# Attention scores in groups of four heads: fp32 row groups in place of restacked three-part rows

## The chip, the cores and the metric

The kernel runs on one core of one Trainium2 chip. The metric is the device time of one execution in microseconds (us), less is better. A median over runs is given where several were timed. Engines: TensorE (PE; its weight loads are PEld), VectorE (DVE), ScalarE (ACT), GpSimd (POOL), and the DMA queue that SyncE (SP) issues.

## The reference

A batch of 16 sequences of 512 tokens, width 512, goes through one conditioned transformer layer and a rotation, all in fp32:

```
x = LN(src) * (1 + scale_b) + shift_b            # scale, shift from a time step
q, k, v = x Wq + bq, x Wk + bk, x Wv + bv        # 16 heads of 32
s = q k^T / sqrt(32) + bias[b, h]                # bias: 16 x 16 x 512 x 512, 268 MB
s[mask] = -inf;  p = softmax(s)
x = x + (p v) Wo + bo
h = LN(x) * g2 + beta2
out = rotate(x + gelu2(h W1 + b1) W2 + b2)       # F = 2048; pairs turned by theta, phi
```

## The kernel before

Three stages follow each other: a setup block (weights split into a high and a low part, `WH` and `WL`, and the modulation), `attention_stage`, and `ffn_stage`. The last two run over the 16 batches; attention writes its context and the modulated x to DRAM (`ctx_dram`, `xmod_dram`), and the FFN stage reads them.

Every engine has its own program with its instructions in an order written out by hand. In `attention_stage` the function `body(mode, b)` is emitted for START, FIRST, MIDDLE (a loop), LAST and END, and walks over 64 slots, one per head j and query tile i of 128 queries (`TL` = 64). Counters on semaphores (`Tally`) say which event of which batch an instruction waits for. Scores run `LEAD` = 6 slots ahead of the transposes.

- Precision: x, the weights, q and k are each split into a high and a low part of reduced fp32 (fp32r). A projection of 128 rows is 12 matmuls of 512 columns (`fill`, L654). For the scores, q and k of each head are restacked: `stacked` holds (hi, hi, lo) of q and (hi, lo, hi) of k under each other, 96 rows, so that one fp32r matmul (L699) gives hi.hi + hi.lo + lo.hi. The restacking is done by DMAs: 12 for q of each group of four heads, two stores and three loads through `k_dram` for k (`stack_rows`).
- Per slot: one score matmul into one of two banks; on VectorE the sum with bias, its row minimum (the negated maximum) and the write to a prob buffer in one instruction (L855, called the max below); exp with its row sum on ScalarE (L749); four transposes (L717) of the probabilities of one head and one key tile, across all four query tiles; a copy of the result to `probT` on ScalarE (even i, L744) or VectorE (odd i, L455).
- After each group of four heads: probs.V in four steps of four heads (L681), fp32, each head in its own 32 columns of the array; the row sums are inverted, widened (L889), transposed and multiplied into the context (L895).
- GpSimd adds the mask to the bias (L609), two tiles at a time, in four half buffers that SP refills; it also makes `maskb` once per batch (L598).
- For the next batch: layer norm statistics and the normalization on VectorE (L801, L813), x transposed, then evicted twice by ScalarE as `XH` and `xf` (L774), and the low part `XL` on VectorE (L866). q and k are evicted as hi on ScalarE (L783) and lo on VectorE (L876), V with its bias on VectorE (L871).
- The FFN stage projects the context with Wo (L1181, plain fp32), adds x and bo, and runs the two FFN products as three-part fp32r matmuls (L1172, L1210).

## Time and profile before

| | |
|---|---|
| median of 3 runs | 3711.62 us (3698.89 to 3714.21) |
| span of the profiled execution, the only time given for it | 3722.1 us |
| TensorE, VectorE, ScalarE, GpSimd busy | 93%, 59%, 44%, 46% |
| mean granted TensorE clock | 0.974 of 2.4 GHz |
| DMA | 525 MB, mean 141 GB/s; 240 to 257 GB/s in the attention stage |
| attention stage, FFN stage | about 1945 us, about 1775 us |

Busy shares count the time in which an instruction of the engine is under way. A matmul's record includes its way through the array, and records overlap; the rate of TensorE is read from the distance of starts. Instructions of one engine run in order.

### The profile page before, as it was taken

Reading aid. Unit: us, or ns where it says so; the run is one execution under the profiler, and the core shown is the slowest. Engines: PE = TensorE matmul, PEld = TensorE weight load, DVE = VectorE, ACT = ScalarE, POOL = GpSimd, SP = SyncE. Lnnn points to the kernel's source line nnn. Section 1 sums busy time; section 2 is a strip of 40 time slices with the busy share of each in tenths; the row PEclk is TensorE's granted clock in tenths of the full one; section 3 lists DMA queues with packets and bytes.
Section 4 is the critical chain, followed back from the end, with each engine's and each line's share of the span. In section 5 each row is a group of like instructions: output and inputs, shape, how many; then the busy total and the mean of one; then the engine's idle time right before and its main releaser. Section 6 shows DMA issues by size and latency. Waiting matters only on the chain. (4 is left out here: it accounts for less than half of the span.)

```text
span 3722.1 us, 58023 instructions
## 1 busy us (share of the span) xinstructions
PE 3463.4 (93%) x17344; PEld 2516.1 (68%) x17344; DVE 2202.4 (59%) x4462; ACT 1635.4 (44%) x3493; POOL 1713.3 (46%) x1131
## 2 busy tenths in 40 slices
PE   4998989899899898999978999999999999999998
PEld 3666656666566666666656777777777777777776
DVE  4887778777887777877754443443444344344443
ACT  3666666666776666666652222222222222222221
POOL 1656566566665656656641322333333233333333
PEclk9999999999999999999987999999999999999999
DMA  5888788888888888878762000100000000000100
GB/s 160 257 248 241 239 245 249 240 247 249 254 256 246 242 247 247 246 233 247 237 212 90 35 26 9 35 34 35 34 35 32 26 12 35 35 35 35 35 6 18
DMA packets 296179, 525.06 MB, mean 141 GB/s; under 512 B 36672, under 2 KB 44864, under 8 KB 295488
## 3 DMA queue, kind: packets, MB, share of 16 engines
q1 hardware_dynamic: 296000, 522.90, 45.9%
q8 instruction: 85, 1.39, 0.2%
q14 instruction: 94, 0.77, 0.1%
HBM read 388.56 MB, written 83.89 MB: 127 GB/s over the span
## 5 line engine op out<-in xcount | busy, mean ns | idle before, releaser
L609 POOL TENSOR_TENSOR biasm<-biasm,maskb 128x1024 f32<-128x1024 f32 x512 | 1099.3, 2155 | 725.5 <-DMA biasm<-in_fside_Bx16xSxS_dram 723.7
L1265 POOL TENSOR_TENSOR g_lo<-g,g_hi 128x512 fp32r<-128x512 f32 x256 | 331.8, 1296 | 1071.5 <-ACT g_hi L1238 1071.5
L1292 DVE SCALAR_TENSOR_TENSOR gate<-ps_h,b_all,gate 128x512 f32<-128x512 f32 x256 | 192.1, 750 | 821.2 <-ACT gate L1228 821.2
L699 PE MATMUL ps_score<-k_rows,q_rows 96*128 96x512 f32 x1024 | 506.1, 494 | 59.4 <-DVE negmax L855 37.5
L1238 ACT ACTIVATE g_hi<-g 128x512 fp32r<-128x512 f32 x256 | 161.9, 633 | 751.3 <-PE ps_out L1210 690.1
L717 PE MATMUL ps_probT<-ident,prob_first 128*128 128x128 f32 x2048 | 407.3, 281 | 77.0 <-DVE probT L455 51.1
L749 ACT ACTIVATE prob_last<-prob_last,negmax 128x512 f32<-128x512 f32 x512 | 367.0, 718 | 173.3 <-DVE negmax L855 171.9
L855 DVE CUSTOM_DVE_ANT_0 prob_first<-ps_score,biasm 128x512 f32<-128x512 f32 x512 | 343.6, 684 | 159.9 <-PE ps_score L699 109.3
L1210 PE MATMUL ps_out<-w_hi,g_hi 128*128 128x512 f32 x1024 | 437.7, 427 | 0.0
L717 PEld LDWEIGHTS ps_probT<-ident,prob_first 128*128 128x128 f32 x2048 | 279.6, 143 | 219.9 <-DVE probT L455 82.9
L744 ACT ACTIVATE probT<-ps_probT 128x512 f32<-128x512 f32 x512 | 303.8, 593 | 268.0 <-PE ps_probT L717 266.8
L749 ACT ACTIVATE prob_first<-prob_first,negmax 128x512 f32<-128x512 f32 x512 | 366.0, 717 | 114.8 <-DVE negmax L855 113.9
L855 DVE CUSTOM_DVE_ANT_0 prob_last<-ps_score,biasm 128x512 f32<-128x512 f32 x512 | 345.8, 684 | 117.0 <-PE ps_score L699 100.1
L1228 ACT ACTIVATE gate<-ps_h,b_half 128x512 f32<-128x512 f32 x256 | 176.2, 688 | 535.8 <-PE ps_h L1172 533.1
L1172 PE MATMUL ps_h<-h_hi,w_hi 128*128 128x512 f32 x1024 | 407.9, 398 | 2.8 <-DVE h_lo L1335 1.4
L699 PEld LDWEIGHTS ps_score<-k_rows,q_rows 96*128 96x128 f32 x1024 | 197.2, 193 | 312.8 <-DVE negmax L855 193.7
L1172 PE MATMUL ps_h<-h_lo,w_hi 128*128 128x512 f32 x1024 | 406.2, 397 | 0.0
L1172 PE MATMUL ps_h<-h_hi,w_lo 128*128 128x512 f32 x1024 | 405.3, 396 | 0.0
L1210 PE MATMUL ps_out<-w_hi,g_lo 128*128 128x512 f32 x1024 | 404.4, 395 | 0.0
L1210 PE MATMUL ps_out<-w_lo,g_hi 128*128 128x512 f32 x1024 | 404.1, 395 | 0.0
L455 DVE COPY probT<-ps_probT 128x512 f32<-128x512 f32 x512 | 347.5, 679 | 92.5 <-issue 46.9
L717 PE MATMUL ps_probT<-ident,prob_last 128*128 128x128 f32 x2048 | 400.6, 278 | 0.0
(132 smaller groups left out, 5801.0 us busy)
## 6 DMA issues: line engine op xcount, KB each, us to landing
biasm<-in_fside_Bx16xSxS_dram SPq DMA_DIRECT2D x512, 512.0 KB, 4.8
k_rows<-k_parts SPq DMA_DIRECT2D x192, 256.0 KB, 4.8
q_rows<-q_hi SPq DMA_DIRECT2D x512, 64.0 KB, 4.3
xn<-in_x_dram SPq DMA_DIRECT2D x16, 1024.0 KB, 7.6
modulated_t<-xf SPq DMA_DIRECT2D x64, 256.0 KB, 2.8
k_parts<-k_hi SPq DMA_DIRECT2D x64, 256.0 KB, 4.1
k_parts<-k_lo SPq DMA_DIRECT2D x64, 256.0 KB, 4.4
q_rows<-q_lo SPq DMA_DIRECT2D x256, 64.0 KB, 4.6
```

What stands on the lines that cost most here:

```text
L455: copy(probT[:, j % GH, i, :], ps_probT[:, i % 2, :]).then_inc(done.sem, 1)
L609: pool.tensor_tensor(tile, tile, maskb[:, 2 * half:2 * half + 2, :], ALU.add).then_inc(masked.sem, 1)
L699: pe.matmul(ps_score[:, n % 2, :], stacked[0][sg % 2][:, sj % GH, si * P:(si + 1) * P], stacked[1][sg % 2][:, sj % GH, :], start=True, sto ...
L717: mm = pe.transpose(ps_probT[:, i % 2, tq * P:(tq + 1) * P], probs(j, tq)[:, i * P:(i + 1) * P], ident[:, :])
L744: copy_out(act, 0, outT_act, lambda o, ps: act.activation(o, ps, ACT.Copy), mode, b, j, i)
L749: e = act.activation(probs(tj, ti), probs(tj, ti), ACT.Exp, bias=negmax[:, tj % 2, ti:ti + 1], scale=-1.0, accum_out=sums[:, (tj // GH) % ...
L855: dve.tensor_tensor_reduce(probs(tj, ti), ps_score[:, n % 2, :], biasm[:, tj % 2, ti, :], -1.0, LOWEST, ALU.add, ALU.min, negmax[:, tj % 2 ...
L1172: mm = pe.matmul(ps_h[:, f % 2, :], w[:, c, f * P:(f + 1) * P], h[:, c, :], start=(c == 0 and n == 0), stop=(c == NC - 1 and n == 2))
L1210: mm = pe.matmul(ps_out[:, t, :], a[:, n % 2, cols], w[:, n, :], start=(n == 0 and k == 0), stop=(n == NF - 1 and k == 2))
L1228: act.activation(gate[:, :], ps_h[:, f % 2, :], ACT.Tanh, bias=b1_half[:, f:f + 1], scale=SIGMOID_RATE / 2).then_inc(tanh_done.sem, 1)
L1265: pool.tensor_tensor(GLO[:, f % 2, :], g[:, :], GHI[:, f % 2, :].bitcast(F32), ALU.subtract)\
L1292: dve.scalar_tensor_tensor(gate[:, :], ps_h[:, f % 2, :], b1_all[:, f:f + 1], gate[:, :], ALU.add, ALU.mult).then_inc(gate_done.sem, 1)
```

## The change

The score matmul is no longer a three-part product of restacked rows. q and k stay unsplit fp32 rows, one tile of 128 rows (four heads of 32) for each group: `qf[g]`, `kf[g]`. A step is now one query tile of four heads (a quad, 16 per batch). Its four scores are four fp32 matmuls, each with the 32 rows of its head and so in its own row group of the array, each into its own bank (`ps_score` has four), with one semaphore event for all. The next quad's scores are issued first in a step, after all four maxima of the quad before have been taken.

Other parts of it:
- `stacked`, `hi`, `lo`, `k_dram` and all restacking DMAs are gone. q is evicted once by ScalarE, k once by VectorE.
- Probabilities are held per quad (`prob`, two buffers); the transposes of one slot take one head and one query tile across the four key tiles. `probT` is doubled (one per group parity), and probs.V runs one key tile per quad, one quad after its group is complete (`PV_LATE`).
- The bias is loaded by query tile for two heads at a time; the mask of one query tile is broadcast over the two heads.
- x transposes and row-sum transposes use the two transpose banks (`ps_turn`) in turn with the probabilities; the projections have one bank (`ps_fill`), each projection in four pieces of three matmuls in four slots (`fill_at`).
- The normalization of x (as add of the negated mean, then multiply) and the low part `XL` move from VectorE to GpSimd, in its queue between the mask additions 18 to 27.
- The bias of V is left out of V and folded into bo in the FFN load (bo + Wo^T bv, 16 products of one column).

```diff
-    k_dram = nc.dram_tensor("k_parts", (2, 2, P, S), F32, kind="Internal").ap()
-    stacked = [[sb(f"{n}_rows{i}", [3 * HD, GH, S], F32R) for i in range(2)] for n in "qk"]
+    qf = [sb(f"q_rows{g}", [P, S]) for g in range(NG)]
+    kf = [sb(f"k_rows{g}", [P, S]) for g in range(NG)]
+    prob = [sb(f"prob{i}", [P, GH, S]) for i in range(2)]
+    probT = [sb(f"prob_t{i}", [P, GH, NT, S]) for i in range(2)]
+    ps_score = bank("ps_score", GH)
+    ps_turn = bank("ps_turn", 2)
+    ps_ctx = bank("ps_ctx")
+    ps_fill = bank("ps_fill")
+    PV_LATE = 1
+    fill_at = {0: ("k", 2), 5: ("q", 2), 10: ("v", 0), 16: ("v", 1), 21: ("v", 2), 26: ("v", 3), 32: ("k", 3), 37: ("q", 3),
+               45: ("k", 4), 50: ("q", 4), 55: ("k", 5), 60: ("q", 5)}
+    x_at = {41: 0, 42: 1, 43: 2, 44: 3}
+    stats_at = (17, 18, 21, 22)
+    AGGR, PICK = 23, 39
+    POW_AT = 18
+    norm_at, split_at = {19: 0, 20: 1, 21: 2, 22: 3}, {24: 0, 25: 1, 26: 2, 27: 3}
+    turn_at = {11: 0, 27: 1, 47: 2, 59: 3}
+    invert_at = {7: 0, 23: 1, 39: 2, 55: 3}
+    ctx_at = {1: 0, 17: 1, 33: 2, 49: 3}
...
 # GpSimd
+            def norm(b, t):
...
+                pool.tensor_scalar(xn[:, t, :], xn[:, t, :], neg_mean[:, t:t + 1], rstd[:, t:t + 1], ALU.add, ALU.mult)\
+                    .then_inc(normed.sem, 1)
+            def split_x(b, c):
+                xf_done.wait(pool, b, c)
+                pool.tensor_tensor(XL[:, c, :], xf[:, c % 2, :], XH[:, c, :].bitcast(F32), ALU.subtract)\
+                    .then_inc(xl_done.sem, 1)
...
+                        if u == POW_AT and mode != LAST:
+                            power(b)
+                        if u in norm_at and mode != LAST:
+                            norm(b, norm_at[u])
+                        if u in split_at and mode != LAST:
+                            split_x(b, split_at[u])
+                        bias_in[u % 4].wait(pool, b, u // 4)
+                        pool.tensor_tensor(tile, tile, maskb[:, n % NT:n % NT + 1, :].broadcast_to([P, 2, S]), ALU.add)\
+                            .then_inc(masked.sem, 1)
...
 # TensorE, one step n
+                        maxed.wait(pe, tb if tn else tb - 1, GH * tn - 1 if tn else TL - 1)
...
+                        for h in range(GH):
+                            rows = slice(HD * h, HD * (h + 1))
+                            mm = pe.matmul(ps_score[:, h, :], qf[g][rows, i * P:(i + 1) * P], kf[g][rows, :],
+                                           start=True, stop=True)
+                        mm.then_inc(scored.sem, 1)
...
+                        for h in range(GH):
+                            head = GH * pg + h
+                            mm = pe.matmul(ps_ctx[HD * h:HD * (h + 1), 0, :], V[:, kt, HD * head:HD * (head + 1)],
+                                           probT[pg % 2][:, h, kt, :], start=(kt == 0), stop=(kt == NT - 1),
+                                           skip_group_check=True)
+                        mm.then_inc(pv_done.sem, 1)
+                    for h in range(GH):
+                        s = GH * n + h
+                        if s in units and mode != END and runs(mode, units[s][0]):
+                            fill(mode, b, *units[s])
+                        if mode in WHOLE:
+                            exped.wait(pe, b, s)
+                            k = place["p", s]
+                            wait_turn_bank(mode, b, k)
+                            for kt in range(NT):
+                                mm = pe.transpose(ps_turn[:, k % 2, kt * P:(kt + 1) * P],
+                                                  prob[n % 2][:, h, kt * P:(kt + 1) * P], ident[:, :])
+                            mm.then_inc(turned.sem, 1)
...
 # ScalarE, slot s = 4 n + h
+                            act.activation(prob[tn % 2][:, h, :], prob[tn % 2][:, h, :], ACT.Exp,
...
+                        if mode in WHOLE and h in (1, 3):
+                            copy_out(mode, b, s - 1)
...
 # VectorE, slot s = 4 n + h
+                        if h == 0:
+                            if n > 0 and mode in WHOLE:
+                                copy_out(mode, b, s - 1)
...
+                            dve.tensor_tensor_reduce(prob[tn % 2][:, h, :], ps_score[:, h, :], biasm[:, tn % 2, h, :],
...
+                        if h == 3 and mode in WHOLE:
+                            copy_out(mode, b, s - 2)
```

## Rows read from the trace of the kernel before

**Rows 1.** Page, span and busy time of TensorE.

```profile
span 3722.1 us, 58023 instructions
...
PE 3463.4 (93%) x17344; PEld 2516.1 (68%) x17344; DVE 2202.4 (59%) x4462; ACT 1635.4 (44%) x3493; POOL 1713.3 (46%) x1131
```

**Rows 2.** The mask conversion by its line: count, min/median/max ns, first and last start.

```profile
L598 POOL TENSOR_SCALAR maskb<-mask_raw x16: 1897/1897/1900, 41.9 to 1812.6; 128x2048 bf16<-128x2048 uint8 x16
```

**Rows 3.** Timeline, TensorE, 1002.5 to 1003.4 us: start, length, engine, line.

```profile
1002.50 0.39 PE L654 MATMUL ps_fill<-x_lo,wq_hi 128*128 128x512 f32 x1
1002.73 0.38 PE L717 MATMUL ps_probT<-ident,prob_first 128*128 128x128 f32 x2
1002.95 0.38 PE L717 MATMUL ps_probT<-ident,prob_last 128*128 128x128 f32 x2
...
1003.40 0.40 PE L654 MATMUL ps_fill<-x_hi,wq_hi 128*128 128x512 f32 x1
```

**Rows 4.** Timeline, TensorE, around two probs.V steps.

```profile
1007.85 0.38 PE L717 MATMUL ps_probT<-ident,prob_last 128*128 128x128 f32 x2
1008.17 1.06 PE L681 MATMUL ps_ctx<-probT,v 128*32 128x512 f32 x8
...
1011.87 1.06 PE L681 MATMUL ps_ctx<-probT,v 128*32 128x512 f32 x8
1012.86 0.50 PE L699 MATMUL ps_score<-k_rows,q_rows 96*128 96x512 f32 x1
```

**Rows 5.** Chain of waits, 160 to 1811 us: total us, times, longest.

```profile
PEld ps_score L699 <- DVE negmax L855: 170.8, 224, 2.0
```

**Rows 6.** Stretches: PE, PEld, DVE, ACT, POOL busy, clock, DMA share, GB/s.

```profile
751.00:869.10 118.10, 109.46 (x648) 75.52 (x646) 91.38 (x210) 80.16 (x189) 74.16 (x35) 0.97 0.83 249
```

**Rows 7.** Timeline, TensorE, the Wo projection of the FFN stage.

```profile
2138.06 3.60 PE L1181 MATMUL ps_y<-ctx,wo 128*128 128x512 f32 x8
```

**Rows 8.** Groups by line: busy us and mean ns, then idle before.

```profile
L609 POOL TENSOR_TENSOR biasm<-biasm,maskb 128x1024 f32<-128x1024 f32 x512 | 1099.3, 2155 | 725.5 <-DMA biasm<-in_fside_Bx16xSxS_dram 723.7
...
L1265 POOL TENSOR_TENSOR g_lo<-g,g_hi 128x512 fp32r<-128x512 f32 x256 | 331.8, 1296 | 1071.5 <-ACT g_hi L1238 1071.5
...
L1260 POOL TENSOR_SCALAR turned_out<-y_b,rot_now 128x128 f32<-128x128 f32 x128 | 111.7, 872 | 90.7 <-DVE rot_now L1287 90.6
...
L813 DVE TENSOR_SCALAR xn<-xn,mean_var,rstd 128x512 f32<-128x512 f32 x64 | 95.3, 1492 | 1.2 <-POOL rstd L593 1.2
...
L866 DVE TENSOR_TENSOR x_lo<-xf,x_hi 128x512 fp32r<-128x512 f32 x64 | 87.3, 1364 | 5.6 <-ACT xf L774 5.6
...
L889 DVE COPY rsum_wide<-sums 128x512 f32<-128x512 f32 x64 | 65.8, 1028 | 0.0
...
L876 DVE SCALAR_TENSOR_TENSOR q_lo<-ps_fill,bqk,q_hi 128x512 fp32r<-128x512 f32 x64 | 47.8, 747 | 33.2 <-ACT q_hi L783 33.1
```

**Rows 9.** Page, DMA issues: KB each, median us to landing.

```profile
biasm<-in_fside_Bx16xSxS_dram SPq DMA_DIRECT2D x512, 512.0 KB, 4.8
```

**Rows 10.** Timeline, VectorE and ScalarE, 1004.1 to 1006.2 us.

```profile
1004.12 0.68 DVE L855 CUSTOM_DVE_ANT_0 prob_first<-ps_score,biasm 128x512 f32<-128x512 f32 x1
...
1004.73 0.68 DVE L455 COPY probT<-ps_probT 128x512 f32<-128x512 f32 x1
...
1004.95 0.71 ACT L749 ACTIVATE prob_first<-prob_first,negmax 128x512 f32<-128x512 f32 x1
...
1005.69 0.60 ACT L744 ACTIVATE probT<-ps_probT 128x512 f32<-128x512 f32 x1
...
1006.18 0.71 ACT L749 ACTIVATE prob_last<-prob_last,negmax 128x512 f32<-128x512 f32 x1
```

**Rows 11.** Timeline, ScalarE, the x evictions ahead of batch 0.

```profile
54.16 0.78 ACT L774 ACTIVATE x_hi<-ps_fill,mod_now 128x512 fp32r<-128x512 f32 x1 [21.40 <-PE ps_fill L639]
...
55.50 0.78 ACT L774 ACTIVATE x_hi<-ps_fill,mod_now 128x512 fp32r<-128x512 f32 x1
```

**Rows 12.** Timeline, TensorE, the first score.

```profile
79.56 0.77 PE L699 MATMUL ps_score<-k_rows,q_rows 96*128 96x512 f32 x1 [5.76 <-DMA k_rows<-k_parts]
```

More of the change, by code:

```diff
@@ L259, in attention_stage @@
     NG = H // GH
+    NQ = NG * NT
     def sb(name, shape, dt=F32):
@@ L416, in runs @@
             return True
-        ahead = f[0] == "x" or (f[0] in "qk" and f[1] >= NG)
+        ahead = f[0] != "v" and f[1] >= NG
         return ahead if mode == START else (not ahead if mode == LAST else False)
-    def slots(mode):
-        heads = range(3) if mode == END else range(H)
-        return [(j, i) for j in heads for i in range(NT)]
-    def completed_at(mode, j, i):
-        return [f for f in order if complete[f] == NT * j + i and runs(mode, f)]
-    def score_tile(mode, b, j, i):
-        n = NT * j + i + LEAD
-        if n < TL:
-            return (b, n // NT, n % NT) if mode in WHOLE else None
-        return (b + 1, (n - TL) // NT, n % NT) if mode in AHEAD else None
@@ L468, in batches, with goes, of_act @@
+    def goes(mode, kind, n):
+        if kind == "p":
+            return mode in WHOLE
+        return mode in AHEAD if kind == "x" else turn_group(mode, 0, n) is not None
+    def of_act(s):
+        return s % 2 == 0
     def batches(eng, body):
@@ L475, in batches @@
         body(END, B)
-    def rows_event(b, g):
-        return (b - 1, 1) if g < 2 else (b, 0)
-    def wait_rows(eng, mode, b, f):
-        kind, n = f
-        if mode == START and n == NG:
-            return
-        prev, pb = (n - 1, b) if n > 2 else (NG + 1, b - 1)
-        if kind == "k":
-            k_stored.wait(eng, pb, prev - 2)
-        else:
-            ahead, g, buf = group_of((kind, prev))
-            for rows in q_rows_in[buf]:
-                rows.wait(eng, *rows_event(pb + ahead, g))
     with nc.Block() as block:
@@ new lines, in body @@
+                for n in quads(mode):
+                    t = score_quad(mode, b, n)
+                    for h in range(GH):
+                        s = GH * n + h
+                        if t is not None and h % 2 == 1:
+                            u = 2 * t[1] + h // 2 + 4
+                            nb, nu = (t[0], u) if u < 2 * NQ else (t[0] + 1, u - 2 * NQ)
+                            if not (mode == LAST and u >= 2 * NQ):
+                                maxed.wait(sp, t[0], GH * t[1] + h)
+                                load_bias(nb, nu)
+                        if s in x_at and mode in AHEAD:
+                            c = x_at[s]
@@ new lines, in wait_fill_bank, with wait_turn_bank @@
+                kind, n = fills[k]
+                fb = b if k >= 0 else b - 1
+                if kind == "v":
+                    v_done.wait(pe, fb, n)
+                else:
+                    (k_done if kind == "k" else q_done).wait(pe, fb, n - 2)
+            def wait_turn_bank(mode, b, k):
+                k -= 2
+                while k >= 0 and not goes(mode, *through[k]):
+                    k -= 2
+                kind, n = through[k]
+                eb = b if k >= 0 else b - 1
+                if kind == "p":
+                    (out_act if of_act(n) else out_dve).wait(pe, eb, n // 2)
+                elif kind == "x":
+                    xf_done.wait(pe, eb, n)
+                else:
+                    rt_out.wait(pe, eb, n)
@@ new lines, in fill @@
+            def fill(mode, b, f, us):
+                kind, n = f
+                for unit in us:
+                    if unit == 0:
+                        wait_fill_bank(mode, b, f)
+                    c, part = unit // 3, unit % 3
+                    if kind == "v":
+                        cols = slice(n * P, (n + 1) * P)
+                        left, right = (XH, XL, XH)[part][:, c, cols], (WH, WH, WL)[part][2][:, c, :]
+                    else:
+                        w = "qk".index(kind)
+                        cols = slice(n % NG * P, (n % NG + 1) * P)
+                        if f == ("k", NG) and part == 0:
+                            xh_done.wait(pe, b, c)
+                            xl_done.wait(pe, b, c)
+                        left, right = (WH, WL, WH)[part][w][:, c, cols], (XH, XH, XL)[part][:, c, :]
+                    mm = pe.matmul(ps_fill[:, 0, :], left, right, start=(unit == 0), stop=(unit == UNITS - 1))
+                if us[-1] == UNITS - 1:
+                    mm.then_inc(proj_done.sem, 1)
@@ L1007, in project_first @@
                     pe.wait_ge(rest_in, 32)
+                    for o in range(NC):
+                        for c in range(NC):
+                            mm = pe.matmul(ps[:, 0, NF + o:NF + o + 1], wo[:, c, o * P:(o + 1) * P], bv_col[:, c:c + 1],
+                                           start=(c == 0), stop=(c == NC - 1))
+                    mm.then_inc(bias_turned, 1)
                     pe.wait_ge(ctx_in, 32)
```

671 lines of the change are left out of this document (277 added, 394 removed).

## The prediction

> **What bounds the kernel now.** The page comes first: one execution of 3722.1 us in which TensorE is busy 93% [rows 1]. Busy is not rate, so I went on to the starts of its instructions. The edit touches the attention stage (and a few small things at its ends), so I read one batch of it. The mask conversion runs once per batch, first at 41.9 and the sixteenth time at 1812.6 us: 15 periods of 118.05 us [rows 2].
>
> What TensorE needs in such a period follows from start-to-start steps. Two transposes take 0.22, so one is 0.11; four of them and a score matmul go from 1002.73 to 1003.40, so a score is 0.67 - 0.44 = 0.23; a projection matmul is 0.23 (1002.50 to 1002.73) [rows 3]. A probs.V step (four heads, two fp32 passes each) lasts 0.99 until the next matmul starts, and the two transposes ahead of it take 0.32 instead of 0.22: 1.09 with both switches [rows 4]. Per batch: 64 scores 14.7, 12 x 12 projection matmuls 33.1, 256 + 16 + 16 transposes 31.7, 16 probs.V steps 17.4. Sum 97. So 21 us of each 118 are stalls, although no engine looks idle for long. The chain of waits says which: over 14 batches the weight load of the scores stood 170.8 us for the max on VectorE, in 224 pieces of up to 2 us [rows 5]. VectorE is busy 91.4 of 118.1 us, ScalarE 80.2, GpSimd 74.2, and the granted clock averages 0.97 [rows 6]: about 6% of the time at 1.2 instead of 2.4 GHz, some 3.5 us lost per batch. TensorE and VectorE hold each other up across two score banks and a one-slot copy-out; that is what can be won, plus nothing else: the FFN half is not touched.
>
> **The change part by part.** Times are per batch unless said.
>
> Scores. 64 three-part matmuls become 16 groups of four fp32 matmuls with 32 contraction rows each, one bank each. The trace has no row-grouped matmul. From below and above: eight fp32 passes that use 32 columns each (probs.V, L681) lie in 1.06 us [rows 4]; eight at full width (L1181) take 3.60 [rows 7]. If the row groups run side by side as the column groups do, a group costs two passes of 0.43 = 0.86, 0.02 for the staggered starts, and one more switch of 0.10: 0.98, 15.7 per batch, +1.0 over now. If they run one after another it is 3.44, +40. I take the lower end, because L681 shows fp32 passes of independent 32-wide tiles starting together, and the four row groups are independent in inputs and banks. In between: if the four 128-column weight loads follow each other a transpose's length (0.11) apart, 0.33 more, 1.3 in all.
>
> The Trainium skill (TensorE: Matmul & The Clock Gate, "Measured speedup vs the span model") reports 3.07x for four row tiles of 512 columns; by that a group would take 1.30 passes' time, as an estimate 0.24 us longer, and the forecast would be 61 us later. It also says (TensorEngine Tiling, "Key Properties") that a change of tiling mode drains the array, which speaks against this change; by that rule the trace agrees, with the 0.10 us at each switch around L681.
>
> No restacking. 12 q DMAs and 2 + 3 k DMAs per group go from SP's queue, some 8 MB per batch of traffic (4 groups of 12 x 64, 3 x 256 and 2 x 256 KB), and so do ScalarE's waits for them. VectorE loses q_lo, and k_lo becomes one k copy from PSUM of about its length; ScalarE loses k_hi. TensorE never waits for it long now, so this is worth nothing by itself in a steady batch.
>
> Norm and split on GpSimd. VectorE loses 95.3 + 87.3 us over 16 batches = 11.4 per batch [rows 8]. GpSimd gains four splits at 1.30 (same form and size as L1265) = 5.2 and four norms. No GpSimd tensor_scalar of 512 contiguous floats is in the trace; from below half of an L1265 add (0.65), from above L1260's 0.87 for 128 strided elements times four (3.5). I take 1.3, nearest in shape: 5.2. GpSimd then needs 74.2 + 10.4 = 85, up to 94, still under TensorE's 98. The add of the mask must come 4.8 (landing) + 2.1 after the buffer is freed [rows 8, 9]; two query tiles are 12 us, so about 4 us of cover are left, and a norm at 3.5 would eat it and cost about 6.
>
> Steps of a query tile of four heads. Busy time per step of the new order, 16 steps a batch: TensorE 98/16 = 6.1. VectorE 91.4 [rows 6] - 11.4 - 3.0 (q_lo, L876) = 77, so 4.8, of which the four maxes (0.61 from start to start) and two copies (0.60) are 3.6 [rows 8, 10]. ScalarE at most 80.2, so 5.0, with exp to copy at 0.74 and copy to exp at 0.49 [rows 6, 10]. The score group waits for all four maxes of the last, but it is issued a whole step before them: scores are in at 1.1, the fourth max ends at 3.6, the second copy at 4.2, and TensorE, which meanwhile has probs.V and up to four projection pieces, asks for that bank at 4.8 to 6.2. So the 21 us of ping-pong go in 14 of 16 steps. What stays, counted step by step: the third step, where ScalarE's q eviction sits ahead of a copy (1.1); the seventh, where V eviction and widening (1.03, L889) push VectorE (0.8) [rows 8]; some 0.7 elsewhere: 2.6.
>
> The x stretch (steps 11 and 12). x transposes now share the two transpose banks, and ScalarE evicts each in two passes, 1.34 a pair [rows 11], before the next exp in its queue. From the start of step 11: exp 0 ends 2.5, q eviction 3.5, exp 1 4.2, copy 4.7; only then is the bank free for x0 (4.8 to 5.2); its pair ends 6.75, exp 2 7.5, x1's pair 8.9, exp 3 9.6, copy 10.1, then the last transpose and x2 to 11.1. In step 12 x3's pair ends 15.5, exp 16.2, copy 16.7, and TensorE leaves at 19.5. Its work in both is 12.0, so 7.5 is lost there. GpSimd's splits fall behind each pair and end at about 18, before their projection piece. With TensorE standing in it, some of this stretch goes to 1.2 GHz as now: 2.
>
> Sum: 98 + 2.6 + 7.5 + 2 = 110.1 against 118.05, so -8.0 per batch, -127 in 16. Ends: the first score stood 5.76 us for k_rows and began at 79.56 [rows 12]; without restacking about 10 earlier. Two more columns and 16 one-column products in the FFN load, where TensorE waits for weights: at most +3. Net -7. Together **-134 us**. The execution profiled spans 3722.1, which becomes 3588; the median is 10.5 lower, so I forecast 3711.6 - 134 = **3578 us**.
>
> **Rivals.**
>
> Rival 1: row groups run one after another. For it: nothing in this trace shows a row group at work. Against: L681. Price 2.56 x 16 = 41 per batch, minus the 2.6 of stalls it hides: 38 x 16 = 614 later, 4190 us, slower. It decides from 1.4 us per group on (134/256 = 0.52 above 0.88). The intermediate case, 0.33 per group, gives +84: 3660.
>
> Rival 2: the whole-step handover. The last max frees four banks at once where two banks alternated before. If the scores of the next step come late behind transposes, one chain goes round per step: scores 1.1, maxes 2.4, copy 0.6, transposes 0.5, probs.V 1.1 and a piece and a half of projection 1.1 make 6.8 against 6.1: 11 per batch, 121, 3755. For it: that very wait is the longest now [rows 5]. Against: the scores stand first in TensorE's step. It decides from 0.5 us per step on.
>
> Rival 3: more is won. If the x stretch is no worse than in the kernel before and the clock stays up, 98 + 5 = 103 per batch: 3465.
>
> Rival 4: it does not do what it says: TensorE's 97 are the floor in both, GpSimd's norms at 3.5 or the mask add late at the x stretch bind, +6: 3674.
>
> **Numbers.** Chances: forecast 0.60 (own range 3510 to 3640), more won 0.12, the intermediate row-group case or rival 4 0.10, handover 0.08, serial 0.10. The range must leave out no more than 2 in 10: 3475 to 3720 leaves the serial case, half the handover and the edge of the third. No change is what lies within 0.5% (18.5 us), about what a measurement of this kernel can tell. Faster 0.76, same 0.05, slower 0.19.
>
> **What would show it.** Right: period of the mask conversion near 110; eight row-grouped passes within about 1.1 us and the next matmul 0.98 after; weight-load waits for the max nearly gone; GpSimd norm near 1.3; TensorE gaps left at the x transposes, behind xf. Wrong: row-grouped passes 0.43 apart each (rival 1); VectorE idle for ps_score before the first of each four maxes while TensorE idles for it too (rival 2); maxes waiting for biasm (rival 4). My count treats each engine's queue as regular; waits that slide over two steps would break it.

## The result, and the profile after

The change makes the kernel slower. The changed kernel takes 3885.95 us (median of 4 runs, 3882.3 to 3893.04), the kernel before 3708.96 (4 runs): the ratio is 1.046, interval 1.043 to 1.049. The forecast was 3578 us.

First the page of the changed kernel: span, and busy time of the engines.

```profile
span 3891.3 us, 59315 instructions
...
PE 3545.2 (91%) x18400; PEld 2395.6 (62%) x18400; DVE 1988.4 (51%) x4287; ACT 1582.8 (41%) x3429; POOL 1835.1 (47%) x1259
```

TensorE, VectorE and ScalarE are all busy for a smaller share than before [rows 1], DMA traffic fell from 525 to 390.64 MB, and yet the span is 169 us longer. Every engine waits more. Where, the mask conversion says (its line: count, durations, first and last start):

```profile
L507 POOL TENSOR_SCALAR maskb<-mask_raw x16: 1897/1897/1900, 54.7 to 1963.4; 128x2048 bf16<-128x2048 uint8 x16
```

15 periods of 127.25 us where there were 118.05 [rows 2] and 110.1 were forecast. The account of the 169 us, from starts of instructions: the first score comes at 64.1 instead of 79.56 [rows 12], -15.5; from the first to the last score it is 2012.6 instead of 1840.1 us, +172.5; from there to the first FFN product 97.9 instead of 86.7, +11.2, of which 6.8 are the one-column products with Wo (2118.98 to 2125.81).

Next the price of the score group. The timeline of TensorE (start, length):

```profile
991.91 0.60 PE L619 MATMUL ps_turn<-ident,prob 128*128 128x128 f32 x4
992.44 1.14 PE L592 MATMUL ps_score<-k_rows,q_rows 32*128 32x512 f32 x8
993.51 1.07 PE L606 MATMUL ps_ctx<-prob_t,v 128*32 128x512 f32 x8
994.50 0.66 PE L619 MATMUL ps_turn<-ident,prob 128*128 128x128 f32 x4
```

The row groups do run side by side: eight passes in 1.14 us. From their start to that of probs.V it is 1.07, here and in 219 of the 256 groups, and never less; the switch ahead of them is 0.09 (992.44 less 991.91 less four transposes of 0.11). That makes 1.16, where 0.98 was forecast. The probs.V step behind them takes 1.00 (994.50 less 993.51), where 1.09 was counted with a switch ahead of it. So TensorE's queue carries 2.16 for the two, not 2.07: 0.09 more per step. From the last of its four starts to the next start, a pass takes 0.51 to 0.52 us in a row group and 0.43 in the column groups of the old and new probs.V.

Then VectorE in the same step:

```profile
993.98 0.69 DVE L773 CUSTOM_DVE_ANT_0 prob<-ps_score,biasm 128x512 f32<-128x512 f32 x1 [0.58 <-PE ps_score L592]
...
995.21 0.69 DVE L719 BATCH_NORM_STATS2 stats<-xn 128x6 f32<-128x512 f32 x1
...
997.01 0.68 DVE L773 CUSTOM_DVE_ANT_0 prob<-ps_score,biasm 128x512 f32<-128x512 f32 x1
...
997.61 0.69 DVE L744 COPY prob_t<-ps_turn 128x512 f32<-128x512 f32 x1
```

and TensorE at its end:

```profile
998.45 0.63 PE L619 MATMUL ps_turn<-ident,prob 128*128 128x128 f32 x4 [0.31 <-DVE prob_t L744]
999.01 1.14 PE L592 MATMUL ps_score<-k_rows,q_rows 32*128 32x512 f32 x8
```

This is a closed loop. The scores start at 992.44; the first max follows 1.54 later, four maxes and two statistics fill VectorE until 997.61, then it copies the transposes of the second head out; that frees the bank for the transposes of the fourth head (998.45), and behind these in TensorE's queue stand the next scores (999.01). Once round: 6.57 us. Whatever VectorE does between two maxes is part of it. A second route runs beside this one: two maxes, two exps and the copy of the first head on ScalarE, which frees the bank for the third head's transposes. Whichever ends last sets the step.

The longest waits from 300 to 1900 us (us in total, times, longest) agree with this:

```profile
ACT prob L669 <- DVE negmax L773: 605.3, 296, 5.4
POOL biasm L520 <- DMA biasm<-in_fside_Bx16xSxS_dram: 471.1, 253, 5.0
DVE prob_t L744 <- PE ps_turn L619: 295.7, 181, 7.5
DVE prob L773 <- PE ps_score L592: 182.3, 166, 2.7
...
PEld ps_turn L619 <- ACT prob_t L652: 167.5, 150, 3.4
...
DVE v L794 <- PE ps_fill L568: 51.5, 46, 1.4
...
DVE prob L773 <- POOL biasm L520: 19.9, 22, 1.5
```

The weight load's wait for the max [rows 5] is gone, as forecast. In its place the maxes wait for scores, the copies for transposes, and the V eviction, which stands between two maxes, for a projection that is not finished. The masked bias is hardly ever late.

The step with the widening shows how one operation grows the loop (timeline, VectorE, and the transposes that waited):

```profile
1002.07 0.69 DVE L794 COPY v<-ps_fill 128x512 f32<-128x512 f32 x1 [0.83 <-PE ps_fill L568]
1002.68 1.98 DVE L805 COPY rsum_wide<-sums 128x512 f32<-128x512 f32 x1
1004.58 0.68 DVE L773 CUSTOM_DVE_ANT_0 prob<-ps_score,biasm 128x512 f32<-128x512 f32 x1
...
1006.65 0.66 PE L619 MATMUL ps_turn<-ident,prob 128*128 128x128 f32 x4 [2.86 <-ACT prob_t L652]
```

The eviction (with 0.83 of waiting) and a widening of 1.98 stand ahead of the last three maxes; the third head's transposes wait for ScalarE's copy, which stands behind the exp of the late second max, and TensorE sits idle for 2.86.

The 1.98 is not the work of the widening. All 64 of them (min/median/max ns):

```profile
L805 DVE COPY rsum_wide<-sums x64: 421/520/2087, 110.1 to 2088.7; 128x512 f32<-128x512 f32 x64
```

Of the 64, 31 start while GpSimd runs nothing, and these take 0.42 to 0.43 us. The other 33 start under a mask addition of GpSimd, and every one of them ends 0.28 to 0.29 us after that addition does: the widening waits for it. From 300 to 1900 us the widenings of step 7 take 1.63 on average and those of step 15 take 1.84, while those of steps 3 and 11 all take 0.42. So GpSimd's additions lengthen the loop too, through VectorE, although the maxes hardly ever wait for their result.

In the table, the distances between the starts of consecutive score groups, worked out from the trace and averaged over 12 batches, for the 16 steps of a batch, with the number of projection pieces (0.70 us of TensorE each) that a step of the changed kernel carries. x is transposed in steps 11 and 12.

| step | 1 | 2 | 3 | 4 | 5 | 6 | 7 | 8 | 9 | 10 | 11 | 12 | 13 | 14 | 15 | 16 |
|---|---|---|---|---|---|---|---|---|---|---|---|---|---|---|---|---|
| pieces | 4 | 3 | 3 | 2 | 4 | 3 | 3 | 2 | 4 | 3 | 1 | 3 | 3 | 3 | 3 | 4 |
| changed kernel | 7.3 | 6.1 | 7.6 | 7.4 | 7.9 | 6.6 | 10.4 | 7.9 | 7.6 | 6.1 | 12.9 | 10.9 | 7.6 | 6.3 | 8.7 | 6.9 |
| e2 below | 7.3 | 6.9 | 7.3 | 5.8 | 6.8 | 6.8 | 7.3 | 5.8 | 6.8 | 7.0 | 11.8 | 10.7 | 7.4 | 6.9 | 7.2 | 6.8 |
| e5 below | 7.4 | 6.9 | 7.3 | 5.8 | 6.8 | 6.8 | 7.2 | 5.8 | 6.8 | 7.0 | 6.3 | 11.2 | 7.6 | 6.9 | 7.2 | 6.8 |

TensorE needs 98 + 16 x 0.09 = 99.4 of each 127.25. So some 28 us are stalls, where the forecast had 12.1: 11.0 in the x steps (23.8 less 12.8 of work), 3.9 in step 7 (10.4 less 6.5), and about 13 in the other 13. The work of a step is 2.16 for scores and probs.V, 1.76 for 16 transposes, its pieces, and 0.44 for each further four transposes (four of x; row sums in steps 3, 7, 12 and 15).

### The profile page after: what moved, and what is told of

It reads as the page before. It is cut to its first block and busy times, and to the rows that moved or that the text cites. A ratio compares the mean times of both kernels' runs of the same rounds, so it can differ in the third digit from the quotient of the medians.

```text
span 3891.3 us, 59315 instructions
## 1 busy us (share of the span) xinstructions
PE 3545.2 (91%) x18400; PEld 2395.6 (62%) x18400; DVE 1988.4 (51%) x4287; ACT 1582.8 (41%) x3429; POOL 1835.1 (47%) x1259
## 2 busy tenths in 40 slices
DMA packets 213632, 390.64 MB, mean 100 GB/s; under 512 B 19776, under 2 KB 27968, under 8 KB 212928
## 5 line engine op out<-in xcount | busy, mean ns | idle before, releaser
L669 ACT ACTIVATE prob<-prob,negmax 128x512 f32<-128x512 f32 x1024 | 732.3, 717 | 761.7 <-DVE negmax L773 760.9
L619 PE MATMUL ps_turn<-ident,prob 128*128 128x128 f32 x4096 | 630.1, 280 | 224.4 <-ACT prob_t L652 154.8
L773 DVE CUSTOM_DVE_ANT_0 prob<-ps_score,biasm 128x512 f32<-128x512 f32 x1024 | 662.1, 685 | 249.2 <-PE ps_score L592 224.2
L619 PEld LDWEIGHTS ps_turn<-ident,prob 128*128 128x128 f32 x4096 | 486.8, 143 | 459.2 <-ACT prob_t L652 190.1
L744 DVE COPY prob_t<-ps_turn 128x512 f32<-128x512 f32 x512 | 352.4, 688 | 436.3 <-PE ps_turn L619 386.6
L592 PE MATMUL ps_score<-k_rows,q_rows 32*128 32x512 f32 x2048 | 322.6, 702 | 0.0
L652 ACT ACTIVATE prob_t<-ps_turn 128x512 f32<-128x512 f32 x512 | 297.3, 581 | 22.2 <-PE ps_turn L619 20.9
L606 PE MATMUL ps_ctx<-prob_t,v 128*32 128x512 f32 x2048 | 296.4, 654 | 0.9 <-DVE rsum_t L816 0.9
L1140 PEld LDWEIGHTS ps_out<-w_hi,g_lo 128*128 128x128 f32 x1024 | 192.8, 188 | 53.7 <-issue 14.4
L1102 PEld LDWEIGHTS ps_h<-h_hi,w_hi 128*128 128x128 f32 x1024 | 192.7, 188 | 53.1 <-issue 4.3
```

The lines of the kernel that those rows point to most:

```text
L592: mm = pe.matmul(ps_score[:, h, :], qf[g][rows, i * P:(i + 1) * P], kf[g][rows, :], start=True, stop=True)
L606: mm = pe.matmul(ps_ctx[HD * h:HD * (h + 1), 0, :], V[:, kt, HD * head:HD * (head + 1)], probT[pg % 2][:, h, kt, :], start=(kt == 0), stop ...
L619: mm = pe.transpose(ps_turn[:, k % 2, kt * P:(kt + 1) * P], prob[n % 2][:, h, kt * P:(kt + 1) * P], ident[:, :])
L652: act.activation(probT[g % 2][:, h, :, i * P:(i + 1) * P], ps_turn[:, k % 2, :].rearrange("p (t q) -> p t q", q=P), ACT.Copy).then_inc(out ...
L669: act.activation(prob[tn % 2][:, h, :], prob[tn % 2][:, h, :], ACT.Exp, bias=negmax[:, tn % 2, h:h + 1], scale=-1.0, accum_out=sums[:, g % ...
L744: dve.tensor_copy(probT[g % 2][:, h, :, i * P:(i + 1) * P], ps_turn[:, k % 2, :].rearrange("p (t q) -> p t q", q=P)).then_inc(out_dve.sem, 1)
```

## The experiments

Ten kernels. Theory L is the loop from scores through the maxes and copies back to the scores; its rivals are the row groups' own price (S), the x stretch (X), and GpSimd's new work (G). The median of the kernel before on the same chip was 3707.4 to 3710.1 in all of them. The changed kernel was not timed again beside them: differences from it use its 3886.

**e1: one pass of reduced fp32 for the scores** (hi parts of q and k only; the low parts are left out of the scores).

```diff
-    qf = [sb(f"q_rows{g}", [P, S]) for g in range(NG)]
-    kf = [sb(f"k_rows{g}", [P, S]) for g in range(NG)]
+    qf = [sb(f"q_rows{g}", [P, S], F32R) for g in range(NG)]
+    kf = [sb(f"k_rows{g}", [P, S], F32R) for g in range(NG)]
```

> The changed kernel with q and k rows kept as reduced fp32 (fp32r), so that each of the four row-grouped score matmuls is one pass instead of two; the scores lose their low parts, all else is the same. Theory (the loop per step is set by a chain scores, four maxes, copy, last transposes, scores, with TensorE's scores on it): one pass of 0.51 us less per step both in the chain and in TensorE's work, 0.51 x 256 = 131 us less than the changed kernel, about 3755. Rival (row-grouped fp32 is itself the loss, some switch or weight load that the pass count does not carry): less than 50 us. Rival (steps are bound on ScalarE or VectorE alone): within 20 us.

Measured: 3732.0 us (9 runs), 1.006 of the kernel before (1.003 to 1.009), 154 less than the changed kernel. The timeline of TensorE:

```profile
900.92 0.51 PE L592 MATMUL ps_score<-k_rows,q_rows 32*128 32x512 f32 x4
901.36 1.07 PE L606 MATMUL ps_ctx<-prob_t,v 128*32 128x512 f32 x8
```

The group takes 0.44 instead of 1.07, and 0.63 x 256 = 161: 154 of it come back, more than the 131 expected. So the scores lie on the path in nearly every step. This alone doesn't tell the loop from TensorE's load, as they are part of both. But even with scores this cheap the kernel is no faster than before, so S is not the cause, only a term.

**e2: VectorE's extras moved to the ends of steps, each projection inside one step.**

```diff
-    fill_at = {0: ("k", 2), 5: ("q", 2), 10: ("v", 0), 16: ("v", 1), 21: ("v", 2), 26: ("v", 3), 32: ("k", 3), 37: ("q", 3),
-               45: ("k", 4), 50: ("q", 4), 55: ("k", 5), 60: ("q", 5)}
+    fill_at = {0: ("k", 2), 4: ("q", 2), 8: ("v", 0), 16: ("v", 1), 20: ("v", 2), 24: ("v", 3), 32: ("k", 3), 36: ("q", 3),
+               48: ("k", 4), 52: ("q", 4), 56: ("k", 5), 60: ("q", 5)}
...
-    stats_at = (17, 18, 21, 22)
-    AGGR, PICK = 23, 39
+    stats_at = (11, 15, 19, 23)
+    AGGR, PICK = 27, 39
...
-    invert_at = {7: 0, 23: 1, 39: 2, 55: 3}
-    ctx_at = {1: 0, 17: 1, 33: 2, 49: 3}
+    invert_at = {6: 0, 14: 1, 38: 2, 54: 3}
+    ctx_at = {3: 0, 19: 1, 35: 2, 51: 3}
```

> The changed kernel with other slots alone: every projection starts with a step and ends with its fourth slot, so its eviction stands behind the four maxes and the copy of its step; statistics, row-sum widening and the context product also move to the fourth slot. No operation is added or left out. Theory (VectorE's extra work and its waits for unfinished projections stand between the maxes of a step, and the chain carries them): the steps that took 7.4 to 10.4 us (steps 3, 4, 7, 9 and 15 of 16 by my reading) fall towards 6.7, some 12 to 16 us per batch, 200 to 250 us less than the changed kernel, 3640 to 3690. Rival (the chain without extras is the bound already, extras hide beside it): within 40 us. Rival (the x stretch carries it): within 60 us, as it is left where it is.

Measured: 3748.0 us (4 runs), 1.012 (1.009 to 1.014), 138 less than the changed kernel, with the same instructions in other slots. That is less than the 200 to 250 that L gave, and well over the 40 and 60 of the rivals: L holds in kind. The period (the mask conversion's line) is 118.06:

```profile
L507 POOL TENSOR_SCALAR maskb<-mask_raw x16: 1897/1897/1900, 54.5 to 1825.4; 128x2048 bf16<-128x2048 uint8 x16
```

The table's second row now has two kinds of step: about 6.8 with four projection pieces, which is within 0.1 of TensorE's own sum (2.16 for scores and probs.V, 1.76 for 16 transposes and 2.8 for the pieces); and 5.8 with none, where TensorE has 3.9 of work. One of the latter, in the timeline:

```profile
819.04 1.14 PE L592 MATMUL ps_score<-k_rows,q_rows 32*128 32x512 f32 x8
...
820.59 0.69 DVE L773 CUSTOM_DVE_ANT_0 prob<-ps_score,biasm 128x512 f32<-128x512 f32 x1 [1.03 <-PE ps_score L592]
...
822.04 0.57 ACT L705 ACTIVATE rsum_t<-ps_turn 128x512 f32<-128x512 f32 x1
...
822.42 0.69 DVE L773 CUSTOM_DVE_ANT_0 prob<-ps_score,biasm 128x512 f32<-128x512 f32 x1
...
823.22 0.58 ACT L652 ACTIVATE prob_t<-ps_turn 128x512 f32<-128x512 f32 x1
823.42 0.69 DVE L744 COPY prob_t<-ps_turn 128x512 f32<-128x512 f32 x1 [0.30 <-PE ps_turn L619]
...
823.86 1.09 PE L619 MATMUL ps_turn<-ident,prob 128*128 128x128 f32 x8 [0.47 <-ACT prob_t L652]
...
824.88 0.71 PE L592 MATMUL ps_score<-k_rows,q_rows 32*128 32x512 f32 x4
```

From the scores it is 1.55 to the first max, VectorE's copy ends at 5.07, the next scores stand at 5.84. Both routes of the loop are in the rows, and here ScalarE's ends last: the transposes at 823.86 wait for its copy (823.22), which came late because ScalarE had first to take the row sums out of a transpose bank (822.04). Both steps without pieces, 4 and 8, follow a transpose of row sums. A step without it, step 10 of e9 below (one matmul per piece), takes 5.59 to 5.60 in each of 12 batches, and in the one read in full (from 499.52) the third head's transposes wait for ScalarE's copy too. A step takes the longer of the two, TensorE's work or the loop; what TensorE spares in a light step is lost, and a full one does not get it.

**e8: the projections' part of e2 alone** (only `fill_at` as above).

> The changed kernel with the first part of e2 alone: only the projections (and so the evictions of k, V and q) move to end with a step; statistics, widening and the context product stay in the slots of the change. If VectorE's waits for unfinished projections between its maxes are the larger part of what e2 took away: 90 us or more of the 138, 3750 to 3800. If the other extra work is: under 50 us, above 3835.

Measured: 3790.0 us (4 runs), 1.022 (1.016 to 1.028): 96 of e2's 138, as expected for the larger part. This part is the k and V evictions that stood between maxes and waited there for their projection; the q evictions on ScalarE move with them and are not told apart. The other 42 are statistics, widening and context product, and in part the wait for GpSimd: a widening takes 1.04 us on average in e8 and 0.61 in e2.

**e5: e2, and x spread over two steps in the projection's bank** (`ps_fill`, which is free then).

```diff
-    x_at = {41: 0, 42: 1, 43: 2, 44: 3}
+    x_at = {41: 0, 43: 1, 45: 2, 47: 3}
...
-                                mm = pe.transpose(ps_turn[:, k % 2, tq * P:(tq + 1) * P], xn[:, tq, c * P:(c + 1) * P],
+                                mm = pe.transpose(ps_fill[:, 0, tq * P:(tq + 1) * P], xn[:, tq, c * P:(c + 1) * P],
```

> The kernel of e2 (evictions at the step's end, 3748) with the x transposes moved from slots 41 to 44 to slots 41, 43, 45 and 47 and from the two transpose banks to the projection bank, which is empty there. Theory (the x stretch costs 22.5 us for 12 of work, because x and the probabilities wait for each other's bank behind ScalarE's double eviction): the two steps fall to some 15 us, 7 per batch, 110 us less than e2, about 3640. Rival (the stretch is long because ScalarE's eight evictions and four exps lie in one queue there, whatever the bank): 20 to 50 us less than e2.

Measured: 3675.6 us (4 runs), 0.990 (0.984 to 0.995): 72 less than e2, between the 110 of the theory and the 20 to 50 of its rival, and faster than the kernel before. Step 11 falls from 11.8 to 6.3; step 12 stays at 11.2.

**e6: e2, and the same slots for x, but in the transpose banks.**

```diff
-    x_at = {41: 0, 42: 1, 43: 2, 44: 3}
+    x_at = {41: 0, 43: 1, 45: 2, 47: 3}
```

> The kernel of e2 with the x transposes at slots 41, 43, 45 and 47 alone, still in the two transpose banks. If the sharing of the banks is the cause of the long x stretch, it stays long: within 40 us of e2 (3710 to 3790). If only the crowding into four slots next to each other is, it gives as much as e5, about 3640.

Measured: 3707.2 us (10 runs), 0.999 (0.996 to 1.001): 41 less than e2, between the two cases expected. Both causes are real: of X's 72, spreading gives 41, and the bank of its own, with the waits that go with it, 31. In the changed kernel the stretch looks like this (TensorE):

```profile
1037.48 0.66 PE L629 MATMUL ps_turn<-ident,xn 128*128 128x128 f32 x4 [1.17 <-ACT prob_t L652]
1039.88 0.66 PE L629 MATMUL ps_turn<-ident,xn 128*128 128x128 f32 x4 [1.31 <-ACT xf L689]
...
1043.26 1.12 PE L619 MATMUL ps_turn<-ident,prob 128*128 128x128 f32 x4 [2.72 <-ACT prob_t L652]
...
1045.16 2.09 PE L592 MATMUL ps_score<-k_rows,q_rows 32*128 32x512 f32 x8
...
1052.87 0.66 PE L619 MATMUL ps_turn<-ident,prob 128*128 128x128 f32 x4 [2.03 <-ACT prob_t L652]
...
1056.15 1.14 PE L592 MATMUL ps_score<-k_rows,q_rows 32*128 32x512 f32 x8
```

TensorE waits for ScalarE's evictions and copies in turn, and the score group at 1045.16 takes 2.09 instead of 1.14, while the granted clock from 1030 to 1055 us is 0.86 on average: the stalls bring some of it to 1.2 GHz.

**e3: scores issued ahead of the last transposes, the copy behind two maxes.**

```diff
                     for h in range(GH):
                         s = GH * n + h
+                        if h == GH - 1:
+                            scores(next_quad(n))
...
 # VectorE
-                        if h == 0:
-                            if n > 0 and mode in WHOLE:
-                                copy_out(mode, b, s - 1)
...
+                        if h == 1:
+                            if n > 0 and mode in WHOLE:
+                                copy_out(mode, b, s - 2)
...
```

> The changed kernel with two places moved: TensorE issues the scores of the next quad before the projection piece and transposes of the fourth slot instead of behind them, and VectorE copies the fourth head's transposes behind the second max of the next step instead of ahead of the first. Theory (the scores are late because they stand behind the last transposes, which wait for a copy that stands behind all four maxes): the chain loses copy 0.6 and transposes 0.5, 1.1 less per step where the chain binds (about 12 of 16 steps), up to 13 us per batch, 100 to 200 us less than the changed kernel, 3690 to 3790. Rival (the chain is not the bound, the extras or the throughput is): within 40 us.

Measured: 3844.9 us (4 runs), 1.038 (1.035 to 1.040): 41 less than the changed kernel, where 100 to 200 were expected and within 40 for the rival. So this test does not show what the last transposes cost in the loop: the move brought waits of its own. The last piece of a projection now stands behind the next scores in TensorE's queue, and the k and V evictions wait 204.5 us for their projections (300 to 1850 us), where they waited 84.8 in the changed kernel (300 to 1900 us). And a wait for the masked bias has come, which was 19.9 above:

```profile
DVE prob L776 <- POOL biasm L520: 135.5, 39, 6.5
```

**e10: e5 and e3 together.** Its diff is the sum of theirs.

> The kernel of e5 (3676) with the two moves of e3 on top: scores issued ahead of the last piece and transposes of a step, and the copy of the fourth head behind the second max. Theory (with the extra work at the step's end, scores issued ahead of it start while VectorE does that work; steps with four pieces stay at TensorE's 6.8, steps without fall from 5.8): 20 to 60 us less, 3615 to 3655, which would equal or beat e4's 3649. Rival (GpSimd's mask additions, for which e5 already waits 91 us, become the bound as in e3, where the wait was 136): within 20 us of e5 or slower.

Measured: 3762.2 us (4 runs), 1.015 (1.010 to 1.019): 87 more than e5, against L's plain reading. Three waits of VectorE grew (300 to 1800 us; in e5 they are 91.4, 55.4 and 29.9 us):

```profile
DVE prob L777 <- POOL biasm L518: 151.6, 47, 5.1
...
DVE k_rows L796 <- PE ps_fill L568: 105.4, 49, 2.5
DVE v L803 <- PE ps_fill L568: 94.8, 52, 1.9
```

The wait for the masked bias is the largest, but it lies wholly in steps 12 and 13, and steps 11 to 13 together take no longer than before (25.3 us, 25.1 in e5). The loss is elsewhere: steps 2, 6, 10 and 14 take 8.0 to 8.2 instead of 6.8 to 7.0, steps 4 and 8 take 6.6 instead of 5.8, and in each of them a k or V eviction waits 1.5 to 2.5 us for its projection (step 16 grows by 0.8 with such a wait, step 7 has one and does not grow). As in e3, the last piece stands behind the next scores, and the maxes stand behind the eviction. This is read from the trace; no run isolates it.

**e9: a third of the projections' matmuls** (8 of the 12 matmuls of each projection of the attention loop are left out; every wait and eviction stays).

```diff
                 for unit in us:
+                    if unit % 3:
+                        continue
...
-                    mm = pe.matmul(ps_fill[:, 0, :], left, right, start=(unit == 0), stop=(unit == UNITS - 1))
+                    mm = pe.matmul(ps_fill[:, 0, :], left, right, start=(unit == 0), stop=(unit == UNITS - 3))
```

> The changed kernel with 4 of the 12 matmuls of each projection (the high parts alone), all waits and evictions the same: 96 x 0.233 = 22.4 us less of TensorE's own work per batch, 358 in all. Theory (each step goes round one chain through VectorE, and TensorE's projection pieces lie beside it, save where VectorE stands waiting for one): clearly less than half comes back, 60 to 170 us, 3720 to 3830, while one pass of the scores, 0.6 per step, came back whole in e1. Rival (TensorE's throughput is the bound, as my forecast had it): 250 us or more, below 3640.

Measured: 3831.2 us (4 runs), 1.033 (1.028 to 1.037). 12 x 8 matmuls of 0.233 are 22.4 us per batch, 358 in all; 55 come back, just under the 60 to 170 expected. If TensorE's work set the time, all of it would. The stretches from 300 to 1900 us (TensorE, its loads, VectorE, ScalarE, GpSimd busy, then the granted clock) of the changed kernel:

```profile
300.00:1900.00 1600.00, 1397.64 (x8633) 815.33 (x8632) 965.93 (x2398) 924.97 (x2204) 992.49 (x524) 0.95 0.49 159
```

and of e9:

```profile
300.00:1900.00 1600.00, 1243.30 (x7561) 659.94 (x7553) 999.58 (x2446) 934.89 (x2247) 1008.18 (x536) 0.88 0.49 161
```

The clock fell from 0.95 to 0.88 as TensorE stood idle more, and this takes part of the gain. How much at most: 0.07 of full speed less is 14% more of the time at 1.2 instead of 2.4 GHz, and half of that lost if TensorE never waited: 0.07 x 124, some 9 us per batch, an estimate. The period is 3.0 shorter (124.2, the mask conversion starts from 54.3 to 1917.4), so with an even clock 12 of the 22.4 would show, no more. Beside e1, where nearly all of 0.63 per step came back, this tells the loop from the load.

**e4: the kernel before, with only its normalization and split moved to GpSimd.**

```diff
 # GpSimd
+                pool.tensor_scalar(xn[:, t, :], xn[:, t, :], neg_mean[:, t:t + 1], rstd[:, t:t + 1], ALU.add, ALU.mult)\
+                    .then_inc(normed.sem, 1)
...
+                pool.tensor_tensor(XL[:, c, :], xf[:, c % 2, :], XH[:, c, :].bitcast(F32), ALU.subtract)\
+                    .then_inc(xl_done.sem, 1)
...
+            norm_at, split_at = {16: 0, 17: 1, 18: 2, 19: 3}, {20: 0, 21: 1, 22: 2, 23: 3}
...
 # VectorE
-                    dve.tensor_scalar(xn[:, t, :], xn[:, t, :], mean_var[:, t, 0:1], rstd[:, t:t + 1],
-                                      ALU.subtract, ALU.mult).then_inc(normed.sem, 1)
...
-                            dve.tensor_tensor(XL[:, n, :], xf[:, n % 2, :], XH[:, n, :].bitcast(F32), ALU.subtract)\
-                                .then_inc(xl_done.sem, 1)
```

> The kernel before with one part of the change alone: the normalization of x and the low part of x go from VectorE to GpSimd. Theory (this part is a gain by itself, 11.4 us per batch less on a VectorE that is busy 91 of 118, and the loss of the change is in the new steps): 50 to 150 us faster than the kernel before, 3560 to 3660. Rival (GpSimd's mask additions come late by it, or the x stretch waits for its splits, and this part carries the loss): slower than the kernel before by 30 to 100 us.

Measured: 3649.3 us (4 runs), 0.985 (0.983 to 0.988). It is the fastest of all, 61 us under the kernel before. Its mask conversion:

```profile
L619 POOL TENSOR_SCALAR maskb<-mask_raw x16: 1897/1897/1901, 54.5 to 1737.3; 128x2048 bf16<-128x2048 uint8 x16
```

A period of 112.2 instead of 118.05. Part of why it pays shows in the kernel before, in the normalizations on VectorE (min/median/max ns):

```profile
L813 DVE TENSOR_SCALAR xn<-xn,mean_var,rstd x64: 534/1710/2469, 41.9 to 1768.8; 128x512 f32<-128x512 f32 x64
```

The 11 of them during which GpSimd runs nothing take 0.53 to 0.54 us; the mean of 1.49 [rows 8] is for the most part waiting for a GpSimd instruction under way. On GpSimd itself, behind its own additions, the same step takes 0.77.

**e7: the changed kernel with normalization and split back on VectorE** (after slots 27, 31, 35, 38 and one slot behind each x transpose).

```diff
+                if s in (27, 31, 35, 38):
+                    t = (27, 31, 35, 38).index(s)
...
+                    dve.tensor_scalar(xn[:, t, :], xn[:, t, :], mean_var[:, t, 0:1], rstd[:, t:t + 1],
+                                      ALU.subtract, ALU.mult).then_inc(normed.sem, 1)
+                if s - 1 in x_at:
...
+                    dve.tensor_tensor(XL[:, c, :], xf[:, c % 2, :], XH[:, c, :].bitcast(F32), ALU.subtract)\
+                        .then_inc(xl_done.sem, 1)
```

> The changed kernel with its normalization and low part of x put back on VectorE (slots 27, 31, 35, 38 and behind each x eviction). Theory (this part of the change was a gain, also in the new steps, as e4 showed in the old ones): 11 us per batch come back onto VectorE, a part of them onto the chain: 60 to 200 us slower than the changed kernel, 3950 to 4080. Rival (GpSimd's splits, for which ScalarE and TensorE wait in the x stretch, were a loss here): faster than 3886 by 30 or more.

Measured: 3977.8 us (4 runs), 1.070 (1.064 to 1.077): 92 slower than the changed kernel, step 11 at 17.8. VectorE's normalizations take 1.25 on average and its splits 1.09, against 0.53 and 0.69 where GpSimd runs nothing. G is refuted from both sides: GpSimd's part of the change is worth 61 in the kernel before and 92 in the changed one. The rest of the change, put on top of e4, costs 3886 less 3649, 237 us.

## Why the prediction was wrong

**The step that failed is "Steps of a query tile of four heads".** It compared mean busy times per step (6.1, 4.8, 5.0) and one chain, "scores are in at 1.1, the fourth max ends at 3.6, the second copy at 4.2, TensorE asks for that bank at 4.8 to 6.2", and concluded that the 21 us of ping-pong go. Three things were wrong with it.
- The chain was priced short and not closed. In e2's light step the first max starts at 1.55, the fourth ends at about 4.1 and the copy at 5.07, and the next scores stand 0.8 behind that, because they are queued behind the last transposes. Loop 5.84 there and 5.59 in e9 where ScalarE has no row sums to take out, against 3.9 plus pieces of TensorE's own.
- It put VectorE's extras (four evictions of k, four of V, statistics, widenings, context products) into a mean. They stand between maxes, so each adds its 0.6 and its own wait to one step's loop. Of some 17 us per batch lost outside the x steps, e2 gives about 8 back by placing alone. And it took the widening at its mean of 1.03, which is 0.42 alone and up to 2.4 under a GpSimd addition.
- It let light steps pay for heavy ones. With one score group in flight they can't: a step costs the larger of loop and work (e2's 5.8 and 6.8).

**Rival 2** named this mechanism: one chain through scores, maxes, copy and transposes, 6.8 per step. It had a chance of 0.08, and its 3755 was below what came, since it left out extras and x (its "121" is a slip: 0.7 in each of 256 steps is 179, and its 3755 has 177). Its "against", that the scores stand first in TensorE's step, was a misreading: first in the step is right behind the last transposes of the step before. Its sign in the profile, maxes idle for ps_score, is there at 182.3 us.

**Scores: the reading was right, the term too small.** Side by side, so rival 1 is refuted. 1.16 for a group instead of 0.98 makes 0.18 x 256 = 46 us on the loop; in TensorE's own sum it is 0.09 x 256 = 23 us, as probs.V took 0.09 less than counted. By e1 nearly all of a group's time sits on the path, so this term was short by 23 to 46 us. The Trainium skill (TensorE: Matmul & The Clock Gate, "Measured speedup vs the span model") has four row tiles of 512 columns at 3.07x. By that, four groups one after another at 0.86 would take 3.44 / 3.07 = 1.12 (an estimate) together; the trace has 1.07, and two passes of 0.43 would be 0.86. The rule was closer than the row I went by.

**The x stretch: right in kind, short in size.** 19.5 + 2 were forecast for steps 11 and 12, 23.8 came (their work is 12.8, not 12.0); the shared banks made ScalarE's pairs and copies take turns, as said; e6 gives back 41, and e5 another 31. **Step 7** was forecast to lose 0.8 and loses 3.9: three late maxes behind an eviction and a widening, which takes 1.63 there on average, 1.2 of it spent waiting for GpSimd.

**Norm and split on GpSimd: right, and the norm cheaper than taken.** The changed kernel's groups (busy us, mean ns):

```profile
L491 POOL TENSOR_TENSOR x_lo<-xf,x_hi 128x512 fp32r<-128x512 f32 x64 | 81.2, 1269 | 170.2 <-ACT xf L689 170.2
...
L486 POOL TENSOR_SCALAR xn<-xn,neg_mean,rstd 128x512 f32<-128x512 f32 x64 | 49.2, 769 | 0.3 <-POOL rstd L479 0.3
```

0.77 instead of 1.3 for a norm, 1.27 for a split (1.30 taken). Rival 4 (GpSimd or the mask too late) did not come; that wait is 19.9 us of 1600. What GpSimd's additions do cost is the time that VectorE's widenings stand behind them, which the forecast did not have.

**No restacking**: no run isolates it in a steady batch, where it was forecast at nothing; the first score came 15.5 us earlier (10 forecast). The ends together give -4 instead of -7, as the stretch to the first FFN product grew by 11.2 where at most 3 was allowed.

**What the repair leaves.** e5 has a period of 113.4 (54.6 to 1755.9): 3.3 over the forecast, 1.4 of it the 0.09 per step of scores and probs.V: with VectorE's extras placed and x spread, the period is close to the one forecast. Of the 69 us won in 15 periods the profiled execution shows 46 (3676.0 less 3722.1): the first conversion comes 12.7 later, behind GpSimd's first norms and splits, and from the last to the end it is 1920.1 instead of 1909.5, 10.6 longer. And the period is no gain of the scores: e4 has 112.2 with the old ones. The best kernel is e4, 3649.3 us; whether better placed steps, or another order for e10, would pass it was not tried.

## What to carry to other kernels

When a group of work is handed over whole, write down the loop it closes, from one group's first instruction to the next's, through every queue, and put each extra instruction and what it waits for on the side of the loop where it stands. A step costs the larger of loop and work, and averages over steps hide that. Then put extras where the engine waits anyway, here behind the last copy of a step. And when a change has several parts, measure the small independent one by itself: moving eight operations per batch from VectorE to GpSimd gained 61 us alone, while everything else cost time even when repaired (e5 3675.6, e4 3649.3). And look at the spread of an operation's times before pricing it by its mean: 0.42 and 1.8 us average to a 1.03 that hardly any instance has.

## What the runs showed of the hardware

- Four fp32 matmuls of 32 contraction rows, each in its own row group and bank, run together, but a pass then takes 0.51 to 0.52 us where one in a column group takes 0.43. In e1 the single pass of reduced fp32 goes on after 0.44. Why the two-pass form is slower wasn't measured.
- VectorE's copy of 128x512 fp32 between SBUF tiles takes 0.42 us alone. Started under a mask addition of GpSimd it ends 0.28 to 0.29 us after the addition, in all 33 such cases of the changed kernel, and takes up to 2.09. VectorE's maxes, which read one operand from PSUM, take 0.67 to 0.69 in all 1024 cases, whatever GpSimd does.
- GpSimd's add-then-multiply of 128x512 fp32 by two columns takes 0.77 us. The same work as subtract-then-multiply on VectorE took 0.53 to 0.54 with GpSimd at rest and 1.49 on average in the kernel before [rows 8].
- Removing TensorE work can lower the clock: 0.95 to 0.88 in e9, and a score group takes 2.07 to 2.09 instead of 1.14 behind a long stall.
